# Each engine's own order at the entry into the feed-forward loop and at its close

## The reference

```python
# cross-attention of one batch
q = 1.0 + elu(query @ Wq.T + bq)
k = where(mask, 0, 1.0 + elu(key @ Wk.T + bk))      # v = value @ Wv.T + bv
q = l2_normalize(q, axis=2)                         # over the sequence
k = l2_normalize(k, axis=3)                         # over the head's 16
out = (q @ (k.T @ v)) @ Wo.T + bo                   # per head

# one feed-forward layer
h = shift_token(x)                                  # second half of the columns one row later
q, k, v = split(h @ wqkv, 3)                        # 8 heads of 64
q = l2norm(q) * q_scale;  k = l2norm(k) * k_scale
q, k = rotary_xpos(q, k)
o = local_attention(q, k, v)                        # windows of 128 rows, one back
x = x + o @ wo
h = shift_token(x)
h = layernorm(h) * g + b
a, gate = split(h @ w1 + b1, 2)
x = x + (a * gelu(gate)) @ w2 + b2
```

## Time and profile before

| | us |
|---|---|
| median of 3 runs | 1258.32 (1258.1 to 1260.74) |
| the profiled execution | 1258.88 |
| its span, first to last instruction | 1257.1 |
| TensorE busy | 1168.3 (93%) |
| VectorE busy | 840.2 (67%) |
| ScalarE busy | 686.9 (55%) |
| GpSimd busy | 587.9 (47%) |
| mean granted clock of TensorE | 0.986 |

### The profile page before, as it was taken

How to read it: one execution, slowest core, us unless ns; L and a number is a source line. 1 busy time by engine, 2 the same in 40 slices (tenths; PEclk the granted TensorE clock), 3 DMA queues, 4 the chain that set the end, 5 groups by cost and what they waited for, 6 DMA issues and landing times.

```text
span 1257.1 us, 20486 instructions
## 1 busy us (share of the span) xinstructions
PE 1168.3 (93%) x6672; PEld 893.2 (71%) x6672; DVE 840.2 (67%) x2443; ACT 686.9 (55%) x1696; POOL 587.9 (47%) x648
## 2 busy tenths in 40 slices
...
DMA packets 31628, 46.11 MB, mean 37 GB/s; under 512 B 4572, under 2 KB 19632, under 8 KB 31536
## 3 DMA queue, kind: packets, MB, share of 16 engines
...
## 4 chain that ended last, share of the span: by engine, by line
PE 53%; issue 20%; POOL 15%; DVE 7%; ACT 4%; DMA 0%; POOLq 0%; DVEq 0%; ACTq 0%
PE psum L1461 33%; POOL probs L625 13%; PE psum L1721 5%; PE psum L1770 4%; PE psum L1755 4%; PE psum L1737 4%; PE psum L1703 2%; ACT hnT_hi L941 1%; DVE stats L994 1%; ACT hnT L941 1%; POOL rn L669 1%; DVE ra L1276 1%; PE psum L1783 1%; DVE rb L1282 1%; DVE xn L1003 1%
## 5 line engine op out<-in xcount | busy, mean ns | idle before, releaser
L625 POOL TENSOR_TENSOR probs<-probs,rden 128x128 f32<-128x128 f32 (+3 forms) x256 | 177.5, 731 | 213.2 <-DVE rden L1055 213.2
L911 ACT ACTIVATE lp<-lp,lneg,rn 128x256 f32<-128x256 f32 (+1 forms) x256 | 143.8, 571 | 17.6 <-DVE lneg L1332 17.4
L780 ACT ACTIVATE probs<-probs,negmax 128x128 f32<-128x128 f32 (+3 forms) x256 | 140.6, 554 | 21.7 <-DVE negmax L1050 21.6
L1043 DVE CUSTOM_DVE_ANT_0 probs<-psum,causal 128x512 f32<-128x512 f32 (+3 forms) x256 | 110.1, 486 | 3.3 <-PE psum L1461 1.4
L669 POOL TENSOR_TENSOR rn<-ss,neg_half 128x8 f32<-128x8 f32 x64 | 107.0, 1671 | 3.8
L1320 DVE CUSTOM_DVE_ANT_0 lp<-psum,local 128x256 f32<-128x256 f32 (+1 forms) x256 | 84.0, 383 | 22.8 <-PE psum L1721 22.8
L660 POOL TENSOR_TENSOR lp<-lp,lrden 128x768 f32<-128x768 f32 x64 | 95.0, 1484 | 0.0
L1461 PE MATMUL psum<-q,k_rest 128*128 128x256 f32 (+2 forms) x256 | 88.9, 358 | 5.4 <-DVE rowmax L1043 3.1
L1527 PE MATMUL psum<-ident,probs 128*128 128x128 f32 x640 | 91.0, 274 | 1.7 <-POOL probs L625 1.6
L1461 PE MATMUL psum<-wqkv_hi,hT_lo 128*128 128x512 f32 x192 | 83.5, 435 | 4.4 <-DVE rb L1282 2.1
L657 POOL TENSOR_TENSOR lp<-lp,lrden 128x128 f32<-128x128 f32 x64 | 26.7, 418 | 128.1 <-DVE lrden L1337 128.1
...
## 6 DMA issues: line engine op xcount, KB each, us to landing
k<-k_round SPq DMA_DIRECT2D x128, 128.0 KB, 2.4
...
w_raw<-in_w SPq DMA_DIRECT2D x2, 1364.0 KB, 6.6
...
```

Of the source, the lines that this page charges most:

```text
L625: ins = pool.tensor_tensor(pr, pr, rden[:, j % 2, h, i:i + 1].broadcast_to([P, TRI[i]]), ALU.mult)
L780: ins = act.activation(pr, pr, ACT.Exp, bias=negmax[:, j % 2, h, i:i + 1], scale=ADH ** -0.5, accum_out=den[:, j % 2, h, i:i + 1])
L911: ins = act.activation(pr, pr, ACT.Exp, bias=lneg[:, u % 2, h, w:w + 1], scale=rn[:, m % 2, w, 0, 2 * j + h:2 * j + h + 1], accum_out=lden ...
L1043: ins = dve.tensor_tensor_reduce(probs[:, j % 2, h, TRI_AT[i]:TRI_AT[i + 1]], bank[:, at:at + TRI[i]], causal[:, S - TRI[i]:S], 1.0, -3e38 ...
```

## The change

The shared lists `cross` and `closing` go. In their place stand four lists for the entry (`ENTRY_PE`, `ENTRY_DVE`, `ENTRY_ACT`, `ENTRY_POOL`) and four for the close, so that each engine has an order of its own there. The entry lists reach further into the loop than `cross` did, to the middle of pass 1 and, on TensorE, to the first output product. The steps run from 1 to 6. The leads in GpSimd's cycle are counted from another pass. The set of items of each engine stays as it was, and between entry and close the lists are the same, with the same banks. A helper `listed` reads the tokens. The norms take their numbers from VectorE's list, and these come out as before.

```diff
+        ENTRY_DVE = ("awo.0 kv.0 norm2.0 keys.0 awo.1 xq.0 KV.0 qadd.0 kv.1 norm2.1 keys.1 kvs.0 awo.2 "
...
-        STEP_POOL = ("bias k3@2 fb2@1 fa3@1 fb3@1 q0@3 k0@3 fa0@2 q1@3 fb0@2 k1@3 norm@1 fa1@2 fb1@2 q2@3 "
-                     "k2@3 fa2@2 q3@3")
+        STEP_POOL = ("bias@-1 k3@1 fb2 fa3 fb3 q0@2 k0@2 fa0@1 q1@2 fb0@1 k1@2 norm fa1@1 fb1@1 q2@2 k2@2 "
+                     "fa2@1 q3@2")
+        CLOSE_PE = ("T.29.0 hnT.6 T.29.1 Sa.31 w1.6.0 Sb.31 w1.6.1 AV.29 T.30.0 w1.6.2 T.30.1 w1.6.3 "
+                    "AV.30 T.31.0 w1.6.4 T.31.1 wo_early.7.0 AV.31 wo_early.7.1 wo.7.0 wo.7.1 w1.6.5 "
...
-        cross = [("awo", 0), ("norm2", 0), ("kv", 0), ("keys", 0), ("awo", 1), ("x1T", 0), ("norm2", 1), ("kv", 1),
...
-        def order_of(cycle):
-
-            middle = [item for m in range(-2, STEPS + 2) for item in step_items(cycle, m) if item not in placed]
-            return cross + middle + closing
-
-        pe_order, dve_order, act_order, pool_order = (
-            order_of(cycle) for cycle in (STEP_PE, STEP_DVE, STEP_ACT, STEP_POOL))
+        def listed(tokens):
+
+            items = []
+            for token in tokens.split():
+                what, *at = token.split(".")
+                at = [int(i) for i in at]
+                items.append(("qkv", *at, what) if what in ("q", "k", "v") else (what, *at))
+            return items
+
+        def order_of(entry, cycle, close):
+
+            entry, close = listed(entry), listed(close)
+            placed = set(entry) | set(close)
+            steps = [item for m in range(1, STEPS - 1) for item in step_items(cycle, m) if item not in placed]
+            return entry + steps + close
+
+        pe_order = order_of(ENTRY_PE, STEP_PE, CLOSE_PE)
...
```

22 lines of the change are left out of this document (14 added, 8 removed), and 38 rows, old and new, of tables (CLOSE_DVE, ENTRY_ACT, ENTRY_DVE, ENTRY_PE).

## The result

| | us |
|---|---|
| median of 4 runs, changed kernel | 1222.41 (1221.09 to 1223.22) |
| median of 4 runs, kernel before | 1258.39 (1258.1 to 1260.74) |
| ratio | 0.9708, 95% interval [0.9693, 0.9723] |
| the profiled execution, and its span | 1221.09, 1219.2 |
| mean granted clock | 0.996 (before 0.986) |

The change is 36.0 us faster.

The account below looks back on a forecast made before the run. The prediction took a chain of mutual waits, no full engine, to bound passes 0 and 1, with further waits at the close. 1258.88 - 19.0 (entry) - 8.5 (close) = 1231.4, stated as 1231, range 1223 to 1246.

Parts of the forecast that it names:

- The hole: Passes 0 and 1: TensorE's 9.3 us wait for VectorE's row maxima goes, with no wait above 3 us in its place.
- cross-attention: Batches 2 and 3, reordered: first q tile at 542.7 against 550.19, VectorE's first tile 9.0 us earlier, 7.5 from TensorE's.
- hnT.7: Close: placed between the halves of w2.6, 5.3 us of matmuls cover its 4.4 us chain, where TensorE waited 3.5.
- The late loads: Loads of wo, w1, w2 wait for y.3: forecast cost 0; as a rival, no gain, 1257 to 1260, chance 0.04.
- behind it, to Tqk.2.0: Entry, after the copy of Tqk.1.3: lists agree and TensorE idles little, so 0.8 us of the gain is taken back.
- close: End of the kernel: waits and half clock cost 10.4 us, of which 8.5 is gained; bounds 3 and 10.4.
- The allowance: VectorE's stretch of passes 0 and 1: the walk of the lists gave waits of 6.4 us, 10 was taken.
- Each term is a wait: Whole change: same instructions and operands, only places move, so no row gets dearer by itself and gains are waits.
- The upper bounds: Most that could be gained: 26 us in passes 0 and 1, the earlier start included, and 10.4 in the close.
- Only the visible holes close: Rival: other waits pass to the next of the cycle; entry gives 9.3 and some 2, close 5: 1243, chance 0.22.
- Everything packs: Rival: entry and close both come near their upper bounds, 26 and 10.4 us: 1222.5, chance 0.08.
- Slower by the clock: Rival: TensorE's clock stays at 1.2 GHz for nearly all of the stretch of passes 0 and 1: 1268, chance 0.04.

Follow-up runs that it names:

- e13: Changed kernel with VectorE's Sa.1 and Sb.1 moved back behind both reciprocals of unit 0, layer 1's tables and q.1.1: 1232.41 us, ratio 0.9793.
- e5: Changed kernel with the old order of cross-attention on all four engines, up to the first tiles: 1230.86 us, ratio 0.9772.
- e6: Changed kernel with hnT.7 put back behind both halves of w2.6 on TensorE and VectorE: 1225.71 us, ratio 0.9733.
- e3: Kernel before with VectorE reading Sa.1 directly behind Sb.0, then layer 1's tables, then the reciprocals: 1258.47 us, ratio 0.9996.
- e12: Kernel before with the lower bound of the sum of squares on GpSimd in place of VectorE: 1259.29 us, ratio 1.0001.
- e8b: Changed kernel with the lower bound of the sum of squares on GpSimd in place of VectorE: 1215.82 us, ratio 0.9648.
- e4: Changed kernel with norms y.2 and y.3 put back directly behind xw.3 on VectorE, y.3 behind y.2 on GpSimd: 1224.14 us, ratio 0.9717.
- e1: Changed kernel with the old order of the close on all four engines, the new entry kept: 1233.30 us, ratio 0.9796.
- e15: Kernel before with VectorE's norms y.2 moved behind soft.2.0 and y.3 behind soft.3.0: 1261.16 us, ratio 1.0026.

## Why the prediction was short

**Right.** The mechanism held: the places, and VectorE as the bound of passes 0 and 1. The hole's own cost in the new list is 10.0 us (e13), cross-attention 8.0 by the ratios (e5: 0.64%) and 9.9 in the entry's trace (forecast 7.5 to 9.0), hnT.7 3.3 (e6). The middle passes all of it on. VectorE ends as the bound, with 79.6 us of work where 79.2 was forecast. The late loads are hidden. The signs named came true, the first three earlier than said: first q tile at 538.19 (said 543), copy of Tqk.1.3 at 627.68 to 628.34 (635), wo issued at 627.70 (630), no wait above 2.6, w1.7 at full clock.

**What failed: the sizes of three terms of the entry's sum.** The table has the gains in us, measured from the first `awo` matmul, so without the 1.9 us that came earlier:

| step | forecast | trace |
|---|---|---|
| VectorE's first tile | 9.0 | 10.8 |
| from there to the copy of Tqk.1.3 | 10.8 | 13.4 |
| behind it, to Tqk.2.0 | -0.8 | 2.9 |
| entry | 19.0 | 27.0 (runs: 25.7) |
| close | 8.5 | 9.1 (runs: 10.6) |

- *Behind the stretch, 3.7 of the 8.0 missed and the largest.* The forecast took 0.8 back, with "Behind this stretch the lists agree"; 2.9 were gained. TensorE's new list has q.2.0 ahead of Tqk.1.3. And since VectorE is full, the copy starts 1.8 us behind the end of the transposes (625.85 to 627.68), while TensorE does k.2.0; before, it followed them at once. So less of TensorE's work is left behind that copy: 200 matmul records in 32.27 us against 212 in 35.14, 2.5 us of busy time, both at a clock of 1.00.
- *The allowance, 2.6.* "A walk leaves out every small slip, so I take 10": VectorE's waits were 7.0 (86.63 - 79.60), near the walk's own 6.4. The allowance of 3.6 was the error; 3.0 of it in waits, less the 0.4 us of work that the forecast had too few, makes the 2.6.
- *Cross-attention, 1.8.* The forecast added 3.3 us of small waits to the 122.5 of work; 2.64 of idle were left (123.18 - 120.54), and TensorE's work was 1.9 less. (The forecast counts y.1 as eight tiles later; in the list it is six. The 1.4 stays the same.)
- *"Each term is a wait."* This premise left out the clock as a part of the entry's gain. TensorE's busy time in the entry fell by 7.5 us in this pair of traces, and by 3.6 to 7.5 over the kernels with the same entry lists; the forecast had the clock as a rival on the other side, and as 2.8 us in w1.7. How much of the 8.0 this makes is not shown: it reaches the length only where TensorE sets it, not in a stretch that VectorE bounds.
- *The upper bounds.* 26 for the entry and 10.4 for the close. The trace has 27.0 in the entry, its 10.8 and 2.9 from outside the stretch that the bound thought of; by the runs it is 25.7, and the close 10.6, each to within 2.4. That either can be passed is not shown.

**The rivals.** "Only the visible holes close" (1243) is out; but its mechanism, a wait that goes and is followed by the next, is real in the old surroundings, where the hole was worth 2.1 of 9.3 (e3) and VectorE's rows 0.4 of 11.4 (e12). "Everything packs" (1222.5, 0.08) met the time to 0.1 us, but by luck in its parts: it had 17 us for the stretch and nothing behind it, and the trace has 13.4 and 2.9. Its argument against, "no stretch as dense as that lasts 80 us in this trace", did not hold: VectorE was busy 92% of 86.6 us. How dense an engine stands in a chain of waits did not tell how dense it could be run. Slower by the clock is out: 0.98 in the stretch.

The rule of the Trainium skill, SBUF — State Buffer, section "SBUF: two separate sides", is that VectorE, with two SBUF inputs, and GpSimd share a port which one holds for its whole instruction. The trace agrees with it beside additions: the sum-of-squares row at 543.64 took 0.77 us and ended at 544.41, where GpSimd's addition of 543.09 ended (544.38), and the one at 596.53, when the GpSimd row then running had 0.1 us left, took 0.17. It does not agree beside the inverse root: in the kernel before, the row at 588.50 took 0.17 in the midst of one that ran from 587.84 to 589.50, and there the measurement decides. The price, though, was there before the change too (16 such rows, 12.22 us before, 12.54 after), and VectorE's work in the stretch was 79.60 where rows of before made 79.2: at most 0.4 us off the gain, not 1 to 5. y.2 and y.3 took 4.92 together where they had taken 2.91, but the tables of layer 1 lost their stretched pair (0.48 each in place of 1.96 and 0.48). Taking the 16 rows off VectorE gave 7.5 us (e8b); how much of that was the port's was not separated.

**Open.** Which of the entry's other moves (TensorE's q.1.1, k.1.1, q.1.2 and Sa.2 ahead, VectorE's order behind Sb.1) carry the part that e3, e4, e5 and e13 don't was not tried one by one. What sets off the two further falls of the clock in the close, with the same lists in e1, e3, e12 (0.94) and in before and e15 (0.96), was not found. The split of the entry's 7.5 us of busy time between clock and anything else was not made; in the cross-attention part 1.9 of it go with a clock that rounds to 1.00 in both.
